# A spectral branch on the turned picture, its channel factor moved into the weights, mirrored parts stored once and read by 128x32 column tiles

## The reference

```python
out0 = gelu(conv1x1(x, in_w, in_b))
x_att = conv1x1(gap(out0), fac_w, fac_b)                 # one number per image and channel
x_fca = abs(ifft2(fft2(out0) * x_att))                   # = |x_att| * |out0|
x_att2 = conv1x1(gap(x_fca), conv_w, conv_b)
x_sca = x_att2 * x_fca
# _fgm(x_sca):
x1 = conv1x1(x, w1, b1)
x2_fft = fft2(conv1x1(x, w2, b2))
enhanced = x2_fft * (1.0 + boost * mask)                 # mask: high frequencies
out = abs(ifft2(x1 * enhanced)) * alpha + x * beta
```

## Time and profile before

| | |
|---|---|
| median of three timed runs | 1813.92 us (1802.71 to 1819.46) |
| profiled execution | 1805.41 us, span 1803.6 us |
| mean granted clock of TensorE | 0.953 |
| PE busy | 1549.4 us (86%) |
| DVE busy | 1364.0 us (76%) |
| ACT busy | 864.2 us (48%) |
| POOL busy | 684.9 us (38%) |

### The profile page before, as it was taken

One profiled execution on the slowest core, in us unless ns is written; L12 is line 12 of the kernel. 1 busy time (PEld: TensorE's weight loads), 2 busy tenths in 40 slices (PEclk: granted clock), 3 DMA queues, 4 the chain that ended last, 5 costly groups with the idle time before them and its releaser, 6 DMA issues.

```text
span 1803.6 us, 32142 instructions
## 1 busy us (share of the span) xinstructions
PE 1549.4 (86%) x11664; PEld 906.3 (50%) x11664; DVE 1364.0 (76%) x2455; ACT 864.2 (48%) x1380; POOL 684.9 (38%) x603
## 2 busy tenths in 40 slices
PE   5789899888989889888998988889888898988884
PEld 3346455464555546445463554546455464555542
DVE  4558778687777878788687777868788786778866
ACT  2344545455454544545455454544545545454533
POOL 3244251634416244251534416134251623416151
PEclk9899999999999999999999999999999999999997
DMA  4011020111102011020111102011020201102020
GB/s 147 1 26 41 26 52 1 43 33 37 39 23 53 0 37 39 25 51 0 43 33 37 39 23 53 0 37 39 25 51 0 58 18 37 39 12 53 0 54 12
DMA packets 19618, 60.23 MB, mean 33 GB/s; under 512 B 6228, under 2 KB 6228, under 8 KB 19204
## 3 DMA queue, kind: packets, MB, share of 16 engines
q1 hardware_dynamic: 19588, 59.83, 13.7%
HBM read 14.04 MB, written 9.02 MB: 13 GB/s over the span
## 4 chain that ended last, share of the span: by engine, by line
DVE 39%; PE 25%; DVEq 16%; issue 7%; ACT 6%; SPq 4%; DMA 3%; ACTq 1%; POOL 0%; POOLq 0%
DVE hv L1090 16%; DVEq L959 7%; DVE nT L929 5%; PE bank L647 5%; PE bank L674 4%; SPq L428 4%; DVE row_max L960 4%; DVEq L965 3%; PE bank L467 3%; PE bank L518 3%; PE bank L489 2%; DMA k_heads<-kC 2%; PE bank L755 2%; DVE score L957 2%; PE bank L577 1%
## 5 line engine op out<-in xcount | busy, mean ns | idle before, releaser
L674 PE MATMUL bank<-act,mats_sb 128*32 128x512 f32 (+11 forms) x2112 | 267.1, 475 | 1.4 <-DVE xs L1026 1.4
L1666 POOL TENSOR_TENSOR score<-score,row_max 128x512 f32<-128x512 f32 x128 | 133.4, 1042 | 306.7 <-DVE row_max L960 305.1
L1350 ACT ACTIVATE fft<-bank 128x512 f32<-128x512 f32 x224 | 168.9, 807 | 125.7 <-PE bank L467 111.8
L1090 DVE SCALAR_TENSOR_TENSOR hv<-hor,mix,hv 128x1024 f32<-128x1024 f32 x128 | 193.8, 1514 | 10.7
L467 PE MATMUL bank<-cons_sb,fft 128*128 128x128 f32 x1280 | 185.4, 306 | 11.8 <-DVE fft L1117 11.8
L1090 DVE SCALAR_TENSOR_TENSOR hv<-ver,mix,hv 128x1024 f32<-128x1024 f32 x144 | 186.9, 1298 | 11.0
L1382 ACT ACTIVATE score<-score 128x512 f32<-128x512 f32 x128 | 80.8, 631 | 225.8 <-POOL score L1666 225.8
L467 PEld LDWEIGHTS bank<-cons_sb,fft 128*128 128x128 f32 x1280 | 172.7, 217 | 31.4 <-DVE fft L1117 17.0
L1677 POOL COPY inv_wide<-row_inv 128x128 f32<-128x128 f32 x128 | 91.8, 717 | 206.7 <-DVE row_inv L966 206.7
L674 PEld LDWEIGHTS bank<-act,mats_sb 128*32 128x32 f32 x2112 | 117.5, 109 | 99.6 <-issue 81.5
L1696 POOL TENSOR_SCALAR hor<-act,cols_sb 128x1024 f32<-128x1024 f32 x16 | 18.0, 1125 | 391.6 <-ACT act L1407 391.6
(11 more groups left out here) (180 smaller groups left out, 2903.9 us busy)
## 6 DMA issues: line engine op xcount, KB each, us to landing
pyr_stack<-pyr SPq DMA_DIRECT2D x192, 144.2 KB, 3.1
x_in<-x_dram SPq DMA_DIRECT2D x16, 512.0 KB, 3.5
k_heads<-kC SPq DMA_DIRECT2D x128, 64.0 KB, 2.4
out_dram<-y_out SPq DMA_DIRECT2D x16, 512.0 KB, 2.8
k_heads<-rel_dram SPq DMA_DIRECT2D x2, 1024.0 KB, 13.0
mats_sb<-mats_dram SPq DMA_DIRECT2D x1, 1978.5 KB, 7.4
z_dram<-z_sb SPq DMA_DIRECT2D x32, 19.1 KB
z_run<-z_dram SPq DMA_DIRECT2D x16, 38.2 KB
```

The lines of the kernel that those rows point to most:

```text
L674: last = pe.matmul(grids[32 * d:32 * d + 32, y0 - 16 * k:y1 - 16 * k, x0:x1], w_pyr[:, d, t], act[:, y0 + dy:y1 + dy, x0 + dx:x1 + dx], st ...
L1090: last = dve.scalar_tensor_tensor(hv[:], src, mix[:, a, k:k + 1], hv[:], ALU.mult, ALU.add)
L1350: return act_.activation(dst, src, ACT.Copy)
L1666: pool.tensor_tensor(score[:, j % 3], score[:, j % 3], row_max[:, j % 3].unsqueeze(2).broadcast_to([P, HEADS, WT]), ALU.subtract)\
```

## The change

Seven edits, all in the spectral branch:

1. `magnitudes` writes `xs` in the order of `act`. What read `xs` as rows now reads it as columns (`xs_turned`), so the whole branch works on the transposed picture, whose spectrum is the transposed one; the high-frequency mask is symmetric in the two.
2. `scaled_input` no longer multiplies `xs`. It multiplies the two weight matrices (128x128) by the channel factor, into `w2_scaled` and `w1_scaled`. `x2_conv` and `pyramid(n, 1)` wait for the first, `r_even` for both.
3. `mirrored` writes each result once: 17 rows of 32 numbers in place of 32.
4. `r_even` and `r_odd` use `part_products`: for each of the 8 pieces of 128 positions, four products with a 128x32 stationary part (one row of the part), each into its own 32 partitions. A row of a part is read twice by address. 32 products each, 128 columns moving.
5. `even_part` moves in front of `keys` on DVE. It needs only `xs` now.
6. `route_weights` gets one 128x1 multiplication, `mix_input` reads `xs` contiguously.
7. `square` writes in order; the matrix `idft_h` is not permuted.

```diff
-    idft = diag(unpack, unpack, unpack, unpack).reshape(P, 4, n)
-    put("idft_h", idft.transpose(0, 2, 1).reshape(P, P))
+    put("idft_h", diag(unpack, unpack, unpack, unpack))
...
+        PARTS = 17 * SIDE
+        w1_scaled, w2_scaled = sb("w1_scaled", C), sb("w2_scaled", C)
...
-        xs_hw = xs.rearrange("p (w h) -> p h w", w=SIDE)
+        xs_turned = xs.rearrange("p (h w) -> p w h", w=SIDE)
...
-                    pe.wait_ge(xs_sb, n + 1)
-                    multiply4(bank[6 + k], xs, k, mat("fgm2")).then_inc(x2_ps, 1)
+                    pe.wait_ge(xs_sb, 2 * n + 1)
+                    multiply4(bank[6 + k], xs, k, w2_scaled[:]).then_inc(x2_ps, 1)
...
+            def part_products(dst, parts, k):
+                for c in range(4):
+                    for q in range(4):
+                        a, r = divmod(4 * (4 * k + c) + q, 2)
+                        at = SIDE * (r if a == 0 else a + 1)
+                        last = pe.matmul(dst[32 * q:32 * q + 32, c * P:(c + 1) * P], parts[:, at:at + SIDE],
+                                         w1_scaled[:], start=True, stop=True)
+                return last
+
             def r_even(n):
                 for k in range(2):
                     pe.wait_ge(xe_sb, n + 1)
+                    pe.wait_ge(xs_sb, 2 * n + 2)
                     pe.wait_ge(h_sb, 2 * n + k + 1)
-                    multiply4(bank[4 + k], xe, k, mat("fgm1")).then_inc(r1_ps, 1)
+                    part_products(bank[4 + k], xe, k).then_inc(r1_ps, 1)
...
-                    multiply4(bank[4 + k], xo, k, mat("fgm1")).then_inc(r2_ps, 1)
+                    part_products(bank[4 + k], xo, k).then_inc(r2_ps, 1)
...
-                dve.tensor_scalar(xs[:], xs[:], vec[:, 6:7], None, ALU.mult).then_inc(xs_sb, 1)
+                dve.wait_ge(r2_ps, 2 * n)
+                dve.tensor_scalar(w2_scaled[:], mat("fgm2"), vec[:, 6:7], None, ALU.mult).then_inc(xs_sb, 1)
+                dve.tensor_scalar(w1_scaled[:], mat("fgm1"), vec[:, 6:7], None, ALU.mult).then_inc(xs_sb, 1)
...
-                d = dst.rearrange("p (a r k) -> p a r k", a=16, r=2)
-                rows_, back, two = xs_hw[:, 1:16], xs_hw[:, 31:16:-1], xs_hw[:, 0:17:16]
-                dve.tensor_tensor(d[:, 1:16, :, 1:32], rows_[:, :, 1:32].unsqueeze(2).broadcast_to([P, 15, 2, 31]),
-                                   back[:, :, 31:0:-1].unsqueeze(2).broadcast_to([P, 15, 2, 31]), op)
-                dve.tensor_tensor(d[:, 1:16, :, 0], rows_[:, :, 0:1].broadcast_to([P, 15, 2]),
-                                   back[:, :, 0:1].broadcast_to([P, 15, 2]), op)
+                d = dst[:, 0:PARTS].rearrange("p (a k) -> p a k", k=SIDE)
+                rows_, back, two = xs_turned[:, 1:16], xs_turned[:, 31:16:-1], xs_turned[:, 0:17:16]
+                dve.tensor_tensor(d[:, 2:17, 1:32], rows_[:, :, 1:32], back[:, :, 31:0:-1], op)
+                dve.tensor_tensor(d[:, 2:17, 0], rows_[:, :, 0], back[:, :, 0], op)
...
             def even_part(n):
-                dve.drain()
-
+                dve.wait_ge(abs_sb, n + 1)
                 dve.wait_ge(r1_ps, 2 * n)
...
+                dve.tensor_tensor(mix[:, 4, 1:2], mix[:, 4, 1:2], vec[:, 6:7], ALU.mult)
...
-                dve.scalar_tensor_tensor(grid(xm[:]), xs_hw, mix[:, 4, 1:2], grid(xm[:]), ALU.mult, ALU.add)\
+                dve.scalar_tensor_tensor(xm[:], xs[:], mix[:, 4, 1:2], xm[:], ALU.mult, ALU.add)\
...
                 norm1(i)
+                even_part(n)
                 keys(i)
                 scaled_input(n)
-                even_part(n)
...
-                act_.activation(xs_hw, act_in, ACT.Abs, accum_out=sums[:, 2:3]).then_inc(abs_sb, 1)
+                act_.activation(grid(xs), act_in, ACT.Abs, accum_out=sums[:, 2:3]).then_inc(abs_sb, 1)
...
-                to = dst.rearrange("c (h j w) -> c j h w", j=CH, w=4)[:, 4 * k:4 * k + 4]
-                return act_.activation(to, ps.rearrange("c (j h w) -> c j h w", j=4, w=4), ACT.Square)
+                return act_.activation(half(dst, k), ps[:], ACT.Square)
```

More of the change, by code:

```diff
@@ L1025, in scaled_input @@
                 dve.drain()
-                dve.tensor_scalar(xs[:], xs[:], vec[:, 6:7], None, ALU.mult).then_inc(xs_sb, 1)
+                dve.wait_ge(r2_ps, 2 * n)
+                dve.tensor_scalar(w2_scaled[:], mat("fgm2"), vec[:, 6:7], None, ALU.mult).then_inc(xs_sb, 1)
+                dve.tensor_scalar(w1_scaled[:], mat("fgm1"), vec[:, 6:7], None, ALU.mult).then_inc(xs_sb, 1)
             def mirrored(dst, op):
-                d = dst.rearrange("p (a r k) -> p a r k", a=16, r=2)
-                rows_, back, two = xs_hw[:, 1:16], xs_hw[:, 31:16:-1], xs_hw[:, 0:17:16]
-                dve.tensor_tensor(d[:, 1:16, :, 1:32], rows_[:, :, 1:32].unsqueeze(2).broadcast_to([P, 15, 2, 31]),
-                                   back[:, :, 31:0:-1].unsqueeze(2).broadcast_to([P, 15, 2, 31]), op)
-                dve.tensor_tensor(d[:, 1:16, :, 0], rows_[:, :, 0:1].broadcast_to([P, 15, 2]),
-                                   back[:, :, 0:1].broadcast_to([P, 15, 2]), op)
-                m = d[:, 0, :, 2:32].rearrange("p r (m u) -> p r m u", u=2)
+                d = dst[:, 0:PARTS].rearrange("p (a k) -> p a k", k=SIDE)
+                rows_, back, two = xs_turned[:, 1:16], xs_turned[:, 31:16:-1], xs_turned[:, 0:17:16]
+                dve.tensor_tensor(d[:, 2:17, 1:32], rows_[:, :, 1:32], back[:, :, 31:0:-1], op)
+                dve.tensor_tensor(d[:, 2:17, 0], rows_[:, :, 0], back[:, :, 0], op)
+                m = d[:, 0:2, 2:32].rearrange("p r (m u) -> p r m u", u=2)
                 dve.tensor_tensor(m, two[:, :, 1:16].unsqueeze(3).broadcast_to([P, 2, 15, 2]),
                                    two[:, :, 31:16:-1].unsqueeze(3).broadcast_to([P, 2, 15, 2]), op)
-                return dve.tensor_tensor(d[:, 0, :, 0:2], two[:, :, 0:17:16], two[:, :, 0:17:16], op)
+                return dve.tensor_tensor(d[:, 0:2, 0:2], two[:, :, 0:17:16], two[:, :, 0:17:16], op)
             def even_part(n):
-                dve.drain()
+                dve.wait_ge(abs_sb, n + 1)
                 dve.wait_ge(r1_ps, 2 * n)
```

## The result

| | before | changed |
|---|---|---|
| median of four runs | 1814.86 us (1802.71 to 1819.46) | 1862.62 us (1855.26 to 1866.76) |
| ratio | | 1.027, 95% interval 1.021 to 1.032 |
| span of the profiled execution | 1803.6 us | 1858.9 us |
| mean granted clock of TensorE | 0.953 | 0.936 |
| instruction transfers (q8) | 18 | 137 |

The account below looks back on a forecast made before the run. No engine bounds it; the chain passes between DVE and PE, 108.2 us an image. Ten full-clock images (11.0), five half-clock (7.0) and the last (3.0) save 21 us: 1790 us forecast, range 1765 to 1812.

Parts of the forecast that it names:

- the one on the column tiles: r_even and r_odd on PE: 64 records each would take 2.0 us, no change; upper bound 3.5 us.
- mix_input, 0.65 us saved: DVE's second mixing pass, reading xs contiguously, saves 0.65 us an image (bounds 0.6 and 1.0); its wait for POOL stays.
- odd_part, 0.85: DVE's odd_part, writing 465 instead of 930 elements, saves 0.85 us an image.
- even_part ahead of keys, 0.3 lost: On DVE before keys: POOL's instructions delay keys 0.3 us in full-clock images (bounds 0 to 0.7), 0 at half clock.
- magnitudes at 0: ACT's magnitudes, written in order, run 0.9 us shorter, but norm1 still waits for POOL: 0 gained, bounds 0 and 0.4.
- Stretch 3: 1136 to 1181 us of one image, PE then DVE's taps: untouched by the change, carries an earlier start through.
- The last image, 3.0: Last image, no swin work, DVE last nearly everywhere: scaling, even_part, mix_input and odd_part together save about 3.0 us.
- the clock takes: Rival, chance 0.10: the half-clock key product comes in every image, 35 us lost against 21 gained: 1828 us.
- The lock takes it back: Rival, chance 0.20: slow column tiles, or even_part losing steps to POOL and delaying keys, cancel the gain: 1803 to 1812 us.
- The clock gives: Rival, chance 0.14: PE's clock no longer falls at the inverse transform behind the even product, 27 us more gained: 1763 us.
- the signs that were to show it: Expected: shorter DVE parts and mix, keys within 0.4 us, no PE idle before r_odd, period down 1.1 to 1.4 us.
- the signs of being wrong: r_odd taking 3 us, PE waiting longer for keys' DMA, or a changed number of half-clock stretches.

Follow-up runs that it names:

- e2: The kernel before with only the column tiles in r_even and r_odd (128x32 products in place of 128x128): 1855.71 us, ratio 1.021.
- e3b: The kernel before with PE's loop over the images written out, without the change: 1826.77 us, ratio 1.008.
- e11: Changed kernel, PE's loop written out, GpSimd's last two vertical convolution taps ahead of the slots, even_part back behind scaled_input: 1779.51 us, ratio 0.982.
- e8: e6 with GpSimd's last two taps of the vertical convolution moved ahead of the spatial attention's slots: 1776.35 us, ratio 0.979, the fastest.
- e7: e3 with GpSimd's last two taps of the vertical convolution moved ahead of the spatial attention's slots: 1786.33 us, ratio 0.986.
- e5: Changed kernel with parts written twice and 128x128 products instead of column tiles, and even_part back behind scaled_input: 1834.3 us, ratio 1.013.
- e6: e5, but with the odd part single and in column tiles; the even part stays doubled and wide: 1811.19 us, ratio 0.9993.
- e9: The kernel before with only GpSimd's last two taps of the vertical convolution moved ahead of the slots: 1817.03 us, ratio 1.002.
- e3: Changed kernel with PE's loop over images 1 to 14 written out: 1825.04 us, ratio 1.006.
- e4: Changed kernel with even_part back behind scaled_input: 1854.19 us, ratio 1.020.

## Why the prediction was wrong

**The step that failed is the one on the column tiles: "no change".** Its pace was right: 2.0 us for 64 records, measured 1.95 and 1.96. But the prediction counted that the records go from 16 to 64, twice, and priced only the time that PE works on them. That they lengthen the loop's body was no term, no bound and no rival, so the range could not hold 1862. By the runs: e2, the tiles alone, +40.5 us in the medians. In its profiled execution the 13 inner images take 3.31 us more each, 43 in all: 2.20 at the jump, 29 in all, and 1.11 beside the work, 14 in all. e3b, with transfers and no jump, lost about as much (1.29 an image), though in other stretches; how much of either is the transfers' and how much the three more half-clock key products' isn't separated. The page of before had the clue: 18 transfers for a kernel of 16 images, from which it could be read that the loop's instructions were being kept, a state that can be lost.

The Trainium skill (Runtime: NRT & Kernel Launch, Instruction fetch mechanics) gives TensorE room for 2048 instructions in blocks of 16 KiB and says that a taken branch to a target outside the two pages at hand stalls. The trace agrees on the stall (1.88 us at the jump) and the 16 KB. It disagrees where the Trainium skill says there that prefetch is purely sequential and that there is no instruction cache: behind the first pass, 1508 and 1604 records are repeated 13 times without one transfer; 1700, still under 2048, are not. The Trainium skill calls the crossing of a block mostly hidden; here the runs are divided, 14 us between e3b and the kernel before, 3 us between e11 and e8.

**mix_input, 0.65 us saved: wrong in sign.** The stride was worth 0.72 us (2.00 against 1.28), near the 0.65 taken. But the prediction kept the wait for POOL as it was (0.35 us, "that stays"), and it rose from some 0.3 us to 1.5 over the two mixes. It had the property right, DVE and POOL shut each other out, applied it to norm1 and even_part, and didn't ask here who comes first: before, DVE, so that POOL waited (1.92 us for L1706). The 0.1 us that it booked for the extra multiplication in route_weights turned that order: that this is what turned it rests on the two groups of kernels above and on e7, where the waits vanish with POOL's instructions; the multiplication was not tried alone, and the turned picture comes and goes with it.

**odd_part, 0.85: right,** 2.09 to 1.29 in the timeline (alone it takes 0.95, against the 1.0 of the prediction) and 0.82 between e5 and e6. With the mix it makes 0.14 us in e6 where 1.4 were forecast; about as much is there once POOL is out of the slots: 1.3 us at full clock between e9 and e8.

**even_part ahead of keys, 0.3 lost: right at keys** (0.25 in the image shown, 0.28 in e7 against e11), and 0.38 short in the slots behind. **magnitudes at 0: right,** L1427 went from 2.03 to 1.06 us and moved nothing that can be seen. **Stretch 3, untouched: right up to the output convolution,** 45.75 and 45.88; the loss at the jump comes right behind it. **The last image, 3.0: mis-sized;** from its input convolution to the end it takes 79.3 against 80.1 us, 0.8 less, and 77.6 (2.5 less) in e3 and e4.

**Of the rivals,** "the clock takes" named a thing that did happen, the key product at half clock in 12 images instead of 5, and 1828. It isn't what decided: e2 has 8 such images, 3 more than the kernel before, and loses 40.5 us. Its price was set too high, too: 3.5 us an image, where the kernel before shows 2.5 between its images with and without it. In the changed kernel the two kinds differ less (111.9 and 111.5 us in the mean of the inner images), but only 3 are at full clock. "The lock takes it back" named the right mechanism at the wrong place: even_part and keys, where it was the mix. "The clock gives" came in at another place than it named: the inverse transform behind the even product is still slow (16 records in 3.45 us in e8 at 1226.02 us), and it is the key product that no longer falls. The timeline of PE in two images of the kernel before, with input convolutions at 1074.99 and 1182.89 us, shows where the clock falls in the second:

```profile
1088.20 0.66 PE L459 MATMUL bank<-cons_sb,nT 128*128 128x128 f32 x4 [1.79 <-DVE nT L929]
...
1088.91 0.38 PE L621 MATMUL bank<-mats_sb,batt_wide 16*128 16x5 f32 x2
...
1196.11 0.77 PE L459 MATMUL bank<-cons_sb,nT 128*128 128x128 f32 x4 [1.79 <-DVE nT L929]
...
1197.02 0.58 PE L621 MATMUL bank<-mats_sb,batt_wide 16*128 16x5 f32 x2
```

The transposes of both start 13.2 us behind the input convolution, with the same 1.79 us idle before them; in the second image they and the small products behind them are already slower, so the key product starts later. The granted clock is 1.00 from 1182.9 to 1195.5 us and 0.50, the lower level, from 1197.5 to 1202. In the table this is why the kernel before, e5, e6 and e9 have over 14.25 us there: in the inner images of the kernel before, those at full clock have 14.23 and those at half clock 14.67. In the changed kernel the stretch varies from 13.56 to 17.2 us, with the key product at half clock at both ends. What makes the clock fall in one image and not in the other is open.

**Of the signs that were to show it,** r_even and r_odd at 1.8 to 2.1 us came true, and L1046 alone near 1.0 (0.95). keys was 0.25 us later in the image shown, but 0.64 later in the mean of the inner images (16.67 us behind the input convolution instead of 16.03). The mix at 1.3 to 1.7 did not come true, nor no idle time before r_odd (0.60 us at 1391.19), nor the shorter period. Of the signs of being wrong two came: PE waits for keys' DMA 37.7 us in all instead of 31.8, and the half-clock images changed in number. DVE's idle time before the scores rose, as foretold, over the span to

```profile
DVE score L969 <- PE bank L519: 140.0, 37, 9.0
```

from 76.2 us. Half of that goes with even_part, which no longer fills the wait, the reason given: with it back in its place (e4) the sum is 107.5. The rest goes with the transfers or the even part's form: it is 79.6 in e6, which has even_part back, none of them, and the doubled even part.

## What to carry to other kernels

When a change cuts products into more and smaller ones inside a hardware loop, count the instructions of the loop's body, and look at the instruction queue's line of the profile's page: few transfers for many passes suggest that the body is resident, and here the change that lost this paid in every pass, most of it at the jump. A saving on VectorE beside GpSimd work can be lost when the order in which the two meet turns; look at who waits there before booking it, and try moving GpSimd's work out of the place. Neither paid alone here (e6 0.999, e9 1.002), both together gave 2.1%, of which a part is that no key product ran at half clock any more.

## What the runs showed of the hardware that was not expected

- A loop body of 1508 or 1604 TensorE records is repeated 13 times behind its first pass with no instruction transfer; with 1700, nine transfers of 16 KB are made in nearly every pass, PE is idle 2.04 us in the mean at each jump, and 3.3 us an image are lost in all.
- Writing out the resident loop of the kernel before (94 transfers instead of 18, no jump) costs 14 us; between e11 and e8 (106 and 19) it is 3.
- Of SP's 128 DMA issues for the keys, 0.59 us in the median, 6 to 8 take over 1.2 us in the kernels with a written-out loop (e3, e3b, e7, e11), 1 to 5 in those with 137 transfers (e4, e2, changed), 1 in those without transfers in the loop.
- A shift of 0.08 us decides who waits: with GpSimd's record 0.03 us ahead of VectorE's, VectorE goes first and GpSimd waits 1.1 us; with it 0.11 us ahead, GpSimd goes first and VectorE waits 0.5 and then 1.1 us.
- A 1024-element pass of VectorE with one input in steps of 128 bytes takes 2.00 us, in order 1.28.
- The same program can run its images in a steady cycle of three (106.7, 107.8, 109.7 us), and in e8, 1.4 us shorter than the full-clock ones in the mean, all at one pace (105.8).
